# Graph layer: the fetch table held in two exact parts for one-pass matmuls, with a smaller ring for the gathers' descriptors

## What is computed

```python
xs = x[src]
deg_w = maximum(seg(edge_weights), 1.0); deg_c = maximum(seg(ones), 1.0)
norm = edge_weights / sqrt(deg_w[src] * deg_w[dst])
gcn   = seg(norm[:, None] * xs) @ Wgcn + bgcn
sage  = x @ Wsage_s + seg(xs) / deg_c[:, None] @ Wsage_n + bsage
agg_w = seg(edge_weights[:, None] * xs)
gin   = ((1 + gin_eps) * x + agg_w) @ Wgin + bgin
gconv = x @ Wgc1 + agg_w @ Wgc2 + bgc
eop   = seg(edge_weights[:, None] * relu(xs + edge_attr)) @ Wedge + bedge
out = layernorm(x + einsum('k,knd->nd', weights, [gcn, sage, gin, gconv, eop]))
```

## Time and profile before

| what | value |
|---|---|
| median of three runs | 2072.93 us (2070.96 to 2073.82) |
| profiled execution, span from its first to its last instruction | 2149.6 us |
| busy in the profiled execution: PE | 1612.0 us (75%) |
| POOL | 1416.1 us (66%) |
| DVE | 949.9 us (44%) |
| ACT | 868.5 us (40%) |
| mean granted clock of TensorE | 0.891 of full speed |

### The profile page before, as it was taken

How to read it: one execution, slowest core, us unless ns; L and a number is a source line. 1 busy time by engine, 2 the same in 40 slices (tenths; PEclk the granted TensorE clock), 3 DMA queues, 4 the chain that set the end, 5 groups by cost and what they waited for, 6 DMA issues and landing times.

```text
span 2149.6 us, 24142 instructions
## 1 busy us (share of the span) xinstructions
PE 1612.0 (75%) x6229; PEld 1037.0 (48%) x6229; DVE 949.9 (44%) x2579; ACT 868.5 (40%) x1181; POOL 1416.1 (66%) x1730
## 2 busy tenths in 40 slices
PE   2006577688889888888888988978988888888435
PEld 1005567545445454555455545545545455445335
DVE  7882465534334343443244433433435253334325
ACT  3784333334434252543254433533435253344003
POOL 6673766676676667667767666666666666666761
PEclk9999865889999899999899998989989999999757
DMA  5111433322222222222222222221222222212421
GB/s 98 25 25 46 132 106 100 83 44 47 58 51 61 48 47 58 52 48 58 44 66 49 55 60 44 54 51 43 68 48 47 54 57 47 59 43 56 103 44 37
DMA packets 81242, 124.52 MB, mean 58 GB/s; under 512 B 28856, under 2 KB 30631, under 8 KB 80009
## 3 DMA queue, kind: packets, MB, share of 16 engines
q0 software_dynamic: 44544, 48.32, 13.4%
q1 hardware_dynamic: 34966, 74.37, 10.9%
q10 hardware_dynamic: 1650, 1.04, 0.2%
HBM read 120.23 MB, written 3.40 MB: 58 GB/s over the span
## 4 chain that ended last, share of the span: by engine, by line
PE 40%; issue 20%; another core or an unknown queue 17%; DVE 11%; ACT 6%; POOL 3%; DVEq 2%; DMA 0%; POOLq 0%; SPq 0%; ACTq 0%
PE psum L1276 26%; PE psum L1257 11%; ACT ring L606 4%; POOL ring L564 3%; DVE ring L1072 2%; DVE sums L1061 2%; DVE early L986 1%; ACT early_x L687 1%; DVE attr L951 1%; DVE early L990 1%; PE psum L1308 1%; PE psum L1337 1%; PE psum L1338 1%; DVEq L1061 1%
## 5 line engine op out<-in xcount | busy, mean ns | idle before, releaser
L564 POOL DMA_INDIRECT ring<-node_table,idx x1280 | 1239.5, 968 | 612.4 <-issue 505.3
L1276 PE MATMUL psum<-table_sb,early_x 128*128 128x455 f32 x2464 | 1040.0, 572 | 46.5 <-issue 33.3
L1276 PEld LDWEIGHTS psum<-table_sb,early_x 128*128 128x128 f32 x2464 | 479.4, 200 | 531.2 <-issue 516.4
L1257 PE MATMUL psum<-ring 128*128 128x120 f32 x2560 | 412.5, 316 | 225.2 <-DVE ring L1072 104.7
L1257 PEld LDWEIGHTS psum<-ring 128*128 128x128 f32 x2560 | 378.3, 226 | 289.8 <-issue 160.1
L687 ACT ACTIVATE early_x<-early,minus_ids 128x256 f32<-128x256 f16 x616 | 408.1, 746 | 239.2 <-remote 144.6
L986 DVE TENSOR_TENSOR early<-psum,digit_hot 128x455 f32<-128x455 f32 x176 | 111.0, 631 | 885.4 <-remote 580.8
L678 ACT ACTIVATE early<-early 128x256 f32<-128x256 f32 x44 | 18.3, 416 | 523.4 <-DVE early L1007 305.0
L653 ACT ACTIVATE ring<-attr 128x512 f32<-128x512 f32 x160 | 99.6, 623 | 319.2 <-DVE attr L951 230.6
L690 ACT ACTIVATE early_x<-early_x,ones 128x1792 f32<-128x1792 f32 x88 | 157.4, 1789 | 2.9
L1257 PE MATMUL psum<-early 128*128 128x120 f32 x576 | 100.8, 328 | 75.8 <-issue 37.0
(11 more groups left out here) (156 smaller groups left out, 611.3 us busy)
## 6 DMA issues: line engine op xcount, KB each, us to landing
attr<-in_edge_attr SPq DMA_DIRECT2D x79, 512.0 KB
ring<-node_table,idx POOLq DMA_INDIRECT x1280
early<-in_edge_attr SPq DMA_DIRECT2D x36, 256.0 KB
src_all<-in_src SPq DMA_DIRECT2D x7, 1024.0 KB
early<-key_rows SPq DMA_DIRECT2D x11, 512.0 KB
early_x<-degree_rows SPq DMA_DIRECT2D x2, 1568.0 KB
early_x<-in_x,early_idx POOLq DMA_INDIRECT x112
node_table<-table_sb SPq DMA_DIRECT2D x1, 1666.0 KB, 6.1
```

The costliest lines, as they stand in the source:

```text
L564: nc.gpsimd.indirect_dma_start(out=feat[:, u, j, D:BLOCK], out_offset=None, in_=table, in_offset=bass.IndirectOffsetOnAxis(ap=idx[:, u, j: ...
L1257: last = nc.tensor.matmul(to[:, 0:3 * WINDOW], features[:, j, 0:2 * D], hots[:, j].rearrange("p k n -> p (k n)"), start=(j == 0), stop=(j ...
L1276: last = nc.tensor.matmul(pick_ps[k % 2].rearrange("p (b c) -> p b c", b=SPLIT), node_hot[:, k, a], table_sb[:, a * SPLIT:(a + 1) * SPLIT, ...
```

## The change

The table is kept in SBUF in two parts. `table_hi` has the entries with their low 12 bits cleared, `table_lo` the rest, which an exact subtraction gives; both have the type float32r and 66 columns for each node (`PART`). `pick_tile` multiplies `node_hot`, now float32r too, by each part in turn and adds all into the same PSUM bank: 14 matmuls of 462 columns in place of 7 float32 matmuls of 455. The full `table_sb` now lies in the second half of `sums` until it is stored and split, and so that half is zeroed later. `key_row16` is written tile by tile, so that ACT reads the keys in a row. The builder's reserve for gather descriptors is 4096 bytes in place of the default 16384.

```diff
+        table_sb = sums[:, 1, 0:NT * TROW].rearrange("p (t d) -> p t d", d=TROW)
+        table_hi, table_lo = (sb(name, [P, NT, PART], F32R) for name in ("table_hi", "table_lo"))
+        top = ring[:, FEATS:FEATS + NT * PART].rearrange("p (t d) -> p t d", d=PART)
-        node_hot = early_flat[:, at_hots:at_hots + HALF * HOT].rearrange(
-            "p (k a e) -> p k a e", k=HALF, a=SPLIT)
+        node_hot = nc.alloc_sbuf_tensor_at("node_hot", [P, HALF, SPLIT, P], F32R, offset=early_at + 4 * at_hots)
...
-            nc.scalar.activation(key_row16[0:BASE], key_row, ACT.Identity, bias=key_bias[0:BASE, 2:3]).then_inc(key_row_step, 1)
+            nc.scalar.activation(key_row16[0:BASE].rearrange("c (j e) -> c e j", e=P), key_row.rearrange("c (e j) -> c e j", j=TILES),
+                                 ACT.Identity, bias=key_bias[0:BASE, 2:3]).then_inc(key_row_step, 1)
...
-            nc.vector.memset(sums[:, 1], 0.0).then_inc(sums_zeroed, 1)
...
+            raw = table_sb[:, :, 0:PART]
+            link(nc.vector.tensor_scalar(top.bitcast(I32), raw.bitcast(I32), TOP_BITS, None, ALU.bitwise_and))
+            nc.vector.tensor_copy(table_hi[:, :, :], top).then_inc(table_split, 1)
+            nc.vector.tensor_tensor(out=table_lo[:, :, :], in0=raw, in1=top, op=ALU.subtract).then_inc(table_split, 1)
+            dve.wait_ge(table_split, 2)
+            dve.wait_ge(x_flip_used, NODE_GROUPS)
+            dve.wait_ge(table_stored, 16)
+            nc.vector.memset(sums[:, 1], 0.0).then_inc(sums_zeroed, 1)
             dve.wait_ge(sums_zeroed, 2)
-            dve.wait_ge(x_flip_used, NODE_GROUPS)
...
+                    pe.wait_ge(table_split, 2)
...
                     for a in range(SPLIT):
-                        last = nc.tensor.matmul(pick_ps[k % 2].rearrange("p (b c) -> p b c", b=SPLIT), node_hot[:, k, a],
-                                                table_sb[:, a * SPLIT:(a + 1) * SPLIT, 0:D + 1],
-                                                start=a == 0, stop=a == SPLIT - 1)
+                        for part in (table_hi, table_lo):
+                            last = nc.tensor.matmul(pick_ps[k % 2], node_hot[:, k, a],
+                                                    part[:, a * SPLIT:(a + 1) * SPLIT].rearrange("p b c -> p (b c)"),
+                                                    start=a == 0 and part is table_hi, stop=a == SPLIT - 1 and part is table_lo)
...
-    nc = bacc.Bacc("TRN2", target_bir_lowering=False, num_devices=1)
+    nc = bacc.Bacc("TRN2", target_bir_lowering=False, num_devices=1, dynamic_dma_scratch_size=4096)
```

More of the change, by code:

```diff
@@ L24 @@
 F32 = mybir.dt.float32
+F32R = mybir.dt.float32r
 BF16 = mybir.dt.bfloat16
@@ L59 @@
 BLOCK = D + TROW
+PART = D + 2
+TOP_BITS = -(1 << 12)
 BITS = WINDOW.bit_length()
@@ L178, in build @@
         inv_count = sb("inv_count", [P, NT])
-        table_sb = sb("table_sb", [P, NT, TROW])
+        table_sb = sums[:, 1, 0:NT * TROW].rearrange("p (t d) -> p t d", d=TROW)
+        table_hi, table_lo = (sb(name, [P, NT, PART], F32R) for name in ("table_hi", "table_lo"))
+        top = ring[:, FEATS:FEATS + NT * PART].rearrange("p (t d) -> p t d", d=PART)
+        assert NT * TROW <= SUMS and NT * PART <= HOTS
         idx = sb("idx", [P, UNROLL, TILES], U32)
+        early_at = -(-nc.sbuf_base // 32) * 32
         early_flat = sb("early_x", [P, EARLY * TILES * D])
@@ L201, in build @@
         ends = np.cumsum(sizes).tolist()
-        sizes_g = (2 * HALF * BLOCK, 2 * HALF * D, HALF * 3 * WINDOW, 2 * SPLIT * (D + 1), CHUNK)
+        sizes_g = (2 * HALF * BLOCK, 2 * HALF * D, HALF * 3 * WINDOW, 2 * SPLIT * PART, CHUNK)
         early = sb("early", [P, max(ends[-1], sum(sizes_g), TURNS * CHUNK // 2)])
@@ L213, in build @@
         key_all = key_all.bitcast(F16)
-        keys_of = [key_all[:, k * CHUNK:(k + 1) * CHUNK].rearrange("p (e j) -> p j e", j=TILES) for k in range(TURN_CHUNKS)]
-        picks = picks.rearrange("p (s c b) -> p s c b", s=2, b=SPLIT)
+        keys_of = [key_all[:, k * CHUNK:(k + 1) * CHUNK].rearrange("p (j e) -> p j e", e=P) for k in range(TURN_CHUNKS)]
+        picks = picks.rearrange("p (s c b) -> p s c b", s=2, b=SPLIT)[:, :, 0:D + 1]
         kept = early[:, 0:TURNS * CHUNK // 2].bitcast(BF16).rearrange("p (k e) -> p k e", k=TURNS)
@@ L253, in build @@
         acc_e, root_ps = bank[7], bank[4]
-        pick_ps = [bank[k][:, 0:SPLIT * (D + 1)] for k in (4, 7)]
+        pick_ps = [bank[k][:, 0:SPLIT * PART] for k in (4, 7)]
         acc_g = bank[3]
@@ L294, in build @@
         root_in, root_out = sem("root_in"), sem("root_out")
-        table_ready, table_stored = sem("table_ready"), sem("table_stored")
+        table_ready, table_stored, table_split = sem("table_ready"), sem("table_stored"), sem("table_split")
         x_flipped, x_flip_used, ones_row = sem("x_flipped"), sem("x_flip_used"), sem("ones_row")
@@ L689, in hot_nodes @@
                     act.wait_ge(node_far, made + 1)
-                    nc.scalar.activation(to, to, ACT.Relu, bias=ones[:, 0:1], scale=-2.0).then_inc(node_hot_made, 1)
+                    nc.scalar.activation(to, to.bitcast(F32), ACT.Relu, bias=ones[:, 0:1], scale=-2.0).then_inc(node_hot_made, 1)
                 def turn(s, begun=True):
@@ L985, in pick @@
                         hot_c = digit_hot[:, bass.ds(c * TILES + half * HALF + k, 1), :].to_broadcast([P, D + 1, SPLIT])
-                        nc.vector.tensor_tensor(out=picks[:, k % 2], in0=pick_ps[k % 2].rearrange("p (b c) -> p c b", b=SPLIT),
+                        nc.vector.tensor_tensor(out=picks[:, k % 2], in0=pick_ps[k % 2].rearrange("p (b c) -> p c b", b=SPLIT)[:, 0:D + 1],
                                                 in1=hot_c, op=ALU.mult).then_inc(pick_taken, 1)
```

## The result

The changed kernel takes 2094.22 us (median of four runs, 2093.53 to 2095.51), the kernel before 2071.94: the ratio is 1.0105, with a 95% interval of 1.0091 to 1.012. The forecast was 2113 us and slower, the range 2045 to 2200. The profiled execution of the changed kernel has a span of 2092.7 us, close to its runs.

A forecast was written before the change was run, and what follows sets the result against it. The prediction took POOL's own pace as the bound: +38 us of pauses and +2 of prologue, with 0 from PE's faster fetch, make +40 on the median 2072.9, so 2113 us; range 2045 to 2200.

The forecast's parts named there:

- The bound: POOL's own pace, 11.48 us a chunk, sets the end for 96% of the loop, though PE is busiest.
- The reserve: POOL's loop: a quarter of the descriptor reserve gives a 0.38 us pause in some 157 of 160 chunks, +38 us.
- Rival (c): POOL's loop: each chunk's pause costs the full 1.53 us, giving 2293 us; chance 0.11.
- Cover of the early gathers: Before the loop: four early pauses hidden by POOL's 25.78 us wait for the table; at most 6 us without it.
- Product waits: POOL's waits for late chunks' products: 0 to 34 us could come back, taken as 0 for the timed runs.
- Rival (b): POOL's first gather of a chunk: real product waits, 34 us, ended by PE's saving; 2040 to 2068 us, chance 0.18.
- The fetch on PE: Picked tiles on PE: 14 float32r matmuls of 0.20 us, 2.8 a tile, saving PE 470 us, 0 on the path.
- rival (d): Picked tiles on PE: float32r matmuls take as long as float32, 0.78 us; PE becomes the bound, beyond 2500 us; chance 0.02.
- The prologue: Work ahead of POOL's loop, and DVE operations beside its first gathers: +2 us in all.
- The key row written with a stride: ACT's write in the prologue: between 0 and +0.9 us over 1.15, delaying the table and POOL's start; +0.9 taken.
- The zeroing of `sums`: DVE, moved from the start to 212.4: 5.32 us, hidden by DVE's later wait for ACT with 2.4 us left.
- The split beside POOL's first gather: Three new DVE operations beside POOL's first gathers lengthen them by 0 to 2.4 us; +1 taken, some 4 by the skill page.

The follow-up runs named there:

- the second execution: The kernel before, run and profiled once more with no edit: 2072.47 us, with a profiled span of 2070.7 us.

## Why the prediction was right, and where it wasn't

**The bound.** Right: POOL's pace, not PE's share. In the run with one matmul of seven PE works 574 us less and the time stays.

**The reserve.** Right: the place is the reserve, its quarter gives a pause in each chunk, and 157 of them sit on the path. The size was off: 0.29 us in place of 0.38, +23.7 in place of +38. The three prices (1.53 whatever is cleared, 0.13 by the gathers cleared, 0.38 by the length of the ring) all left out the place of the pause in the half chunk; the runs show that it counts as much. Rival (c), 1.53 for each, left it out as well. The trace of before has pauses at one place only, so it could not be read there. That 0.38 came near 0.29 is luck: the same rule gives 56 / 113 x 1.53 = 0.76 with 8192 bytes, where 1.28 was measured, and 21 / 113 x 1.53 = 0.28 with 3072, where no pause is seen.

**Cover of the early gathers.** This step failed in part. I let four early pauses vanish under 25.78 us of waiting, a figure of that one long execution; the cover is 6.5 us. Nor are they 1.53 us at most: the three that fall among the early gathers of the changed kernel take 2.0 to 2.2 each over the usual 0.30. They and some longer gathers move the end of the last early gather from 149.5 to 156.2, which uses the cover up, and with the fourth pause at the loop's first gather 1.4 us come through, where I had none.

**Product waits.** I took them for an effect of that execution and priced their relief at 0. Right: 0.9 us. Rival (b) had nothing to win: the second execution has no such waits to take back, and the run with one matmul is no faster.

**The fetch on PE.** The groups and one matmul of the changed kernel:

```profile
L1291 PE MATMUL psum<-table_hi,node_hot 128*128 128x462 f32 x1232 | 510.8, 415 | 0.0
...
L1291 PE MATMUL psum<-table_lo,node_hot 128*128 128x462 f32 x1232 | 487.6, 396 | 0.0
```

```profile
1000.09 0.37 PE L1291 MATMUL psum<-table_hi,node_hot 128*128 128x462 f32 x1
1000.30 0.37 PE L1291 MATMUL psum<-table_lo,node_hot 128*128 128x462 f32 x1
```

They start 0.21 us apart (the 0.37 of each overlap), where I had 0.20: a tile takes 2.95 us, against 2.8, and rival (d) is out. There, from 999.6 to 1003.5, the granted clock is 1.00, the level of 2.4 GHz. From 1008.4 to 1010.8 it is 0.50, that of 1.2 GHz, soon after PE had stood idle for 2.56 us before 1006.18, and the matmuls start 0.39 apart: with PE resting more, part of the gain goes back to the lower clock, and PE is busy for 1252 us, not near 1150.

**The prologue.** Two terms were wrong, in opposite ways. The key row written with a stride takes not 2.06 us but 4.84 (ACT's timeline, against 1.15 in the earlier trace rows):

```profile
131.47 4.84 ACT L623 ACTIVATE sums<-sums,key_bias 36x1024 f16<-36x1024 f32 x1
...
147.75 0.24 ACT L629 ACTIVATE deg_root<-deg_max 128x49 f32<-128x49 f32 x1 [3.13 <-DVE deg_max L912]
```

yet it costs nothing, since ACT then still waits 3.13 us for DVE; the tie at 181.7 in the earlier trace rows was one of that execution too, and in the second profile of before ACT waits 6.84 us there. The zeroing of `sums` was hidden as forecast, but with no slack left (DVE would be ready at 188.17 and ACT's L667 ends at 188.11). The split beside POOL's first gather costs more than my +1 us:

```profile
158.16 3.52 DVE L937 TENSOR_TENSOR table_lo<-sums,ring 128x3234 fp32r<-128x3234 f32 x1
```

```profile
158.49 4.03 POOL L570 DMA_INDIRECT ring<-node_table,idx  x1 [2.05 <-issue]
162.82 0.95 POOL L570 DMA_INDIRECT ring<-node_table,idx  x1 [0.30 <-issue]
```

The gather began 0.33 us behind the subtraction and ended at 162.52, 0.84 after it: it lost 3.06 us, nearly the 3.19 that the subtraction still ran. The Trainium skill, SBUF — State Buffer, "Who interferes with whom", says that a VectorE operation with two inputs in SBUF and a GpSimd operation that reads SBUF block each other wholly; this pair agrees. The some 4 us that I estimated from that page, there for copies, casts and scalar operations, were nearer than the 1 us from row. In the changed kernel the other two steps of the split cost nothing that can be told apart: beside the first, from 152.85 to 156.36, two gathers took 0.94 each, beside the second POOL stood in its pause, and the early gather of 1.99 us at 151.8 is there without them too, in the kernel before with 4096 bytes (1.99 at 151.94). The second step, the cast, does cost where a gather runs beside it. In the run with 30 picked chunks and 6144 bytes one began inside the cast and took 2.16 us, and the next lost 2.2 to the subtraction (DVE, then POOL):

```profile
157.01 2.05 DVE L936 CAST table_hi<-ring 128x3234 fp32r<-128x3234 f32 x1
```

```profile
157.72 2.16 POOL L570 DMA_INDIRECT ring<-node_table,idx  x1 [0.30 <-issue]
160.18 3.13 POOL L570 DMA_INDIRECT ring<-node_table,idx  x1 [0.30 <-issue]
```

So of +40, 38 + 2, the parts measured are +23.7 for the pauses, +1.4 before the loop, +3 for the split, and about -6 for other gathers that are lengthened less, which I hadn't in the sum and whose cause no run shows.

## What to carry to other kernels

Busy shares say which engine works most, not which one is waited for: the pace of one repeated step on each engine, quiet stretches first, tells the bound, and freeing another engine pays only once work is moved onto it (138 us here with 30 picked chunks and 6144 bytes, against 7 without the move with 4096 and 2 with 8192). The reserve for gather descriptors is a tuning parameter, and not one where more is better: try three or four sizes, and look in the timeline at where in the loop the pause falls. Before durations of a prologue or of waits are used as cover, see that the profiled execution's span is near the runs' time.

## What was not expected of the hardware

- A smaller reserve can be faster. The gathers' pauses cost 45.5 us in the loop with 4096 bytes, 50 with 8192, 15.0 with 12288, 21.8 with 16384, and none that can be seen with 3072, 5120 and 6144.
- ACT writing 1024 float16 values with a stride took 4.84 us in place of 1.15, while the earlier trace rows has a strided float32 write of as many at 2.06. The reader of these keys gained: L694 takes 493 ns in the mean, where L687 of the kernel before took 746 with a strided input.
- A gather that began inside a VectorE subtraction with both inputs in SBUF waited it out: 4.03 us in place of 0.97. In all four runs with the split table it ended 0.82 to 0.84 us behind the subtraction (4.03, 3.12, 4.03 and 3.13 us), and the two gathers that began inside the cast ended 0.81 and 0.84 behind that.
